# First attention of a four-layer kernel: the mixing matmuls go ahead of the scores, and GpSimd scales half of the probabilities

## The reference, cut to what matters

```
ln_out = ln(x)
q, k, v    = fp8-rounded linear of ln_out;  q, k per head of 128: layer norm     # "core"
qx         = fp8-rounded linear of ln_out, layer norm per head                    # "cross"
kx, vx     = linear of cond (fp32), kx: layer norm per head
scores = q . k / sqrt(128) ; p = softmax(scores) ; out = p . v                    # 16 heads, 8 key groups
cat = [core, xout] -> clamp, round to fp8 -> linear to 256 features               # added to x
```

## Time and profile before

| | |
|---|---|
| median of 3 runs | 1504.31 us |
| the profiled execution | 1502.7 us |
| its span | 1500.9 us |
| PE busy over the span | 1437.8 us (96%) |
| DVE / ACT / POOL busy | 877.0 / 768.6 / 526.4 us |
| first attention | from the start to about 460 us |

### The profile page before, as it was taken

One profiled execution on the slowest core, in us unless ns is written; L12 is line 12 of the kernel. 1 busy time (PEld: TensorE's weight loads), 2 busy tenths in 40 slices (PEclk: granted clock), 3 DMA queues, 4 the chain that ended last, 5 costly groups with the idle time before them and its releaser, 6 DMA issues. The chain is left out here.

```text
span 1500.9 us, 22370 instructions
## 1 busy us (share of the span) xinstructions
PE 1437.8 (96%) x7006; PEld 1040.2 (69%) x7006; DVE 877.0 (58%) x1923; ACT 768.6 (51%) x2123; POOL 526.4 (35%) x522
## 2 busy tenths in 40 slices
PE   6999999999989999999999999999997999999998
PEld 5677777788875555557878888866764666665656
DVE  5798988899875242333464545455677555553322
ACT  5888888999982211110234444444357655553210
POOL 2767677877761000000533333322111333321000
PEclk9999999999999999999999999999999999999999
DMA  5301000200006511112100000000232000011120
GB/s 204 118 6 64 5 5 1 97 1 1 2 1 265 180 53 49 49 50 91 67 1 1 0 1 1 15 15 6 102 150 97 1 1 1 1 30 43 47 69 17
DMA packets 21880, 71.67 MB, mean 48 GB/s; under 512 B 3922, under 2 KB 6354, under 8 KB 19076
## 3 DMA queue, kind: packets, MB, share of 16 engines
q1 hardware_dynamic: 13556, 57.38, 10.4%
q10 hardware_dynamic: 8208, 12.87, 2.8%
HBM read 69.01 MB, written 1.22 MB: 47 GB/s over the span
## 5 line engine op out<-in xcount | busy, mean ns | idle before, releaser
L1282 ACT ACTIVATE l0f_silu<-bank 128x512 f32<-128x512 f32 x48 | 28.5, 597 | 198.9 <-PE bank L1206 183.0
L948 POOL TENSOR_TENSOR l0a_head_rstd<-l0a_head_var,all_minus_half 128x4 f32<-128x4 f32 x96 | 99.6, 1042 | 18.2 <-DVE l0a_head_var L666 18.2
L1385 DVE TENSOR_TENSOR l0f_product<-l0f_silu,bank 128x512 f32<-128x512 f32 x48 | 32.9, 687 | 124.3 <-ACT l0f_silu L1282 124.2
L920 POOL TENSOR_TENSOR l0a_stepped<-l0a_y,l0a_m 128x512 f32<-128x512 bf16 x64 | 73.8, 1153 | 89.1 <-DVE l0a_m L644 87.5
L484 PEld LDWEIGHTS bank<-l0a_k_t,l0a_q_t 128*128 128x128 f32 x512 | 63.7, 191 | 39.7 <-ACT l0a_q_t L832 35.3
L846 ACT ACTIVATE l0a_work<-bank,l0a_neg_max 128x128 f32<-128x128 f32 x256 | 90.3, 372 | 1.2 <-DVE l0a_neg_max L679 1.2
L1218 PEld LDWEIGHTS bank<-all_weights_a,l0f_hidden 128*128 128x128 f32 x384 | 72.9, 190 | 25.3 <-issue 17.0
L1814 DVE TENSOR_TENSOR all_weights_a<-bank,all_cols 128x512 f32<-128x512 f32 x64 | 43.9, 690 | 77.6 <-PE bank L1649 46.2
L1218 PE MATMUL bank<-all_weights_a,l0f_hidden 128*128 128x256 f32 x384 | 88.9, 379 | 0.0
L2407 PE MATMUL bank<-l3a_f_xn_t,all_weights_b 128*128 128x512 f32 x192 | 86.2, 594 | 0.0
L890 ACT ACTIVATE l0a_work<-l0a_work,l0a_row_inv 128x128 f32<-128x128 f32 x256 | 82.4, 411 | 6.2 <-DVE l0a_row_inv L683 5.9
(11 more groups left out here) (443 smaller groups left out, 3760.3 us busy)
## 6 DMA issues: line engine op xcount, KB each, us to landing
l0f_spread<-l0f_weights ACTq DMA_DIRECT2D x32, 192.0 KB, 2.7
all_weights_a<-in_l_w_q SPq DMA_DIRECT2D x2, 2048.0 KB, 13.8
l0f_spread<-l0f_weights ACTq DMA_DIRECT2D x32, 128.0 KB, 2.8
all_weights_b<-in_l_e_gate_up SPq DMA_DIRECT2D x1, 3200.0 KB, 10.4
all_weights_b<-in_l_e_gate SPq DMA_DIRECT2D x1, 3072.0 KB, 10.0
all_weights_a<-in_l_e_up SPq DMA_DIRECT2D x4, 768.0 KB, 6.7
all_weights_a<-in_l_e_down SPq DMA_DIRECT2D x1, 3072.0 KB, 15.2
l3a_spread<-l3f_weights SPq DMA_DIRECT2D x10, 256.0 KB, 3.4
```

The costliest lines, as they stand in the source:

```text
L920: done = g.tensor_tensor(stepped[:, 0:n], value, step, ALU.add)
L948: g.tensor_tensor(head_rstd[:, m % 2, :], head_var[:, m % 2, :], res.minus_half[:, 0:HU], ALU.pow)\
```

## The change

Two edits. On PE, `mix` comes before `score` within the odd steps. And for a = 0 and a = 3 of every tile the scaling of the probabilities is one POOL instruction on 128 x 512, with `row_inv` broadcast along the row, in place of four ACT instructions. It keeps its step (s+6, that is step 7 for a = 0, and step 5 of the next tile for a = 3). ACT adds a wait for the count of POOL's scaling before that of a = 1.

```
+        POOL_SCALED = (0, 3)
...
-            march(VTS, STEPS, [(turn_probs, later(at_query, 7)), (score, later(at_query, 4)),
-                               (mix, later(at_query, 8)), in_tile(F_TILE, turn_first, F_TURN),
+            march(VTS, STEPS, [(turn_probs, later(at_query, 7)), (mix, later(at_query, 8)),
+                               (score, later(at_query, 4)), in_tile(F_TILE, turn_first, F_TURN),
...
             def scale_probs(b, a):                                   # ACT
+                if a in POOL_SCALED:
+                    return
                 inv_ready.wait(act, inv_ready.at(b, a + 1))
+                if a - 1 in POOL_SCALED:
+                    probs_ready.wait(act, probs_ready.at(b, a))
...
+            def scale_probs(b, a):                                   # POOL
+                if a not in POOL_SCALED:
+                    return
+                inv_ready.wait(g, inv_ready.at(b, a + 1))
+                probs_ready.wait(g, probs_ready.at(b, a))
+                pr = heads(probs[:, a % 2, :])
+                g.tensor_tensor(pr, pr, along(row_inv[:, a, :], P), ALU.mult).then_inc(probs_ready.sem, 1)
...
-            march(VTS, STEPS, [(round_mixed, later(at_query, 9)), (rstd, later(at_norm, 1)), in_tile(F_ROWS_TILE, first_rstd, F_ROWS[0:1]),
+            march(VTS, STEPS, [(round_mixed, later(at_query, 9)), (rstd, later(at_norm, 1)), (scale_probs, later(at_query, 6)),
+                               in_tile(F_ROWS_TILE, first_rstd, F_ROWS[0:1]),
                                in_tile(0, out_low_first, OUT_FIRST_LOW), (quantise, [4, 6, 8]),
```

## The result

The changed kernel took 1547.34 us (median of 4 runs, 1546.90 to 1551.51) against 1504.43 for the kernel before: ratio 1.0295, 95% interval 1.0274 to 1.0317, or +43 us where +38 was forecast. The profiled execution is the longest of the four, 1551.51 us, so its trace stands some 4 us behind the median.

What follows compares the result with a forecast made beforehand. PE was taken to bound the cross tiles and DVE's packed timeline the core tiles. Losses of 13 us (cross), 4.5 and 3.5 (tiles 8, 9), 15 (tiles 10 to 14) and 2 made +38, 1541 us; range 1512 to 1562.

Steps and rivals of the forecast that it cites:

- the timeline of DVE is packed: Core tiles: DVE runs from one rounding to the next without a wait, in a tile of 24.9 us.
- ACT's relief at nothing: Attention tiles: taking 2.6 us a tile from ACT gains nothing, since ACT is not the bound.
- rival (C): Attention tiles: ACT's load causes PE's waits for q_t, so less of it gains some 10 us, 1493 us; chance 0.08.
- The place of the scaling: Core tile, step 5: POOL's scaling of a = 3 starts right behind the quantising, takes 1.04 us, making PE 3.30 us late.
- PE's lateness: Core tile: late transposes delay step 7's row max by 3.1 us, so DVE stands still 2.7 us more.
- PE was to wait once a tile: Expected trace sign: PE's weight loads wait for POOL's new scaling once a tile, about 3 us.
- The hold: Core tiles: POOL's large instruction blocks DVE's 16-bit instructions, 0.6 us more a tile at most.
- The order at 0: Mix ahead of score on PE: taken as 0 in cross and core tiles, between 16 us lost and 10 gained.
- the 5.65 us: Core tile: time from PE's step 6 transposes to the earliest row max of step 7, in the new order.
- The bound of 16 us: Largest loss from mix ahead of score: 0.5 us on all 32 query units of the core tiles.
- The sum: First 460 us: 13 + 4.5 + 3.5 + 15 + 2 = +38 us, giving 1541 us; what follows unchanged.
- cross tiles 27.5: Expected trace sign: cross tiles take 27.5 us in the changed kernel.

Runs made afterwards that it cites:

- spare multiply: Kernel before plus an unread GpSimd multiply of the same size at the two new places, ScalarE still scaling: 1521.8 us, ratio 1.0119.
- scaling ahead of the quantising: GpSimd scales a = 0 and 3, score ahead of mix, two quantisings moved one step later, against the kernel before: 1523.4 us, ratio 1.0130.
- order alone: Kernel before with only mix put ahead of score on PE, all four scalings still on ACT: 1512.8 us, ratio 1.0062.
- wait alone: Kernel before plus an unread 4-column GpSimd power at the two places, PE's transposes of a = 0 and 3 waiting for it: 1531.6 us, ratio 1.0179.
- spare small instruction: Kernel before plus an unread GpSimd power of 128x4, about 1.0 us long, at the two new places: 1503.8 us, ratio 0.9998.
- relief alone: Kernel before with a = 0 and 3 scaled by no engine, PE's transposes of them waiting for the exponentials only: 1505.4 us, ratio 1.0014.
- scaling alone: Changed kernel without its second edit: GpSimd scales a = 0 and 3, score ahead of mix; against the kernel before 1534.5 us, ratio 1.0204.

## Why the prediction was right

**What bounds the kernel.** "In the core tile the timeline of DVE is packed" is true only with two things that I had not counted. Of the 24.9 us 3.4 are hold, so the list by itself is shorter. And there is a loop of the same length: DVE's rounding, POOL's two rounding instructions and rstd, DVE's normalise and next rounding, 6.2 us per query unit (375.74 to 381.90 in the earlier trace rows). Once in each core tile DVE waits for it, also in tile 13, just behind the stretch that I had read as free of waits:

```profile
385.46 0.69 DVE L674 TENSOR_TENSOR l0a_work<-bank,l0a_head_rstd 128x512 f32<-128x512 f32 x1 [0.32 <-POOL l0a_head_rstd L948]
```

With rstd 1.3 us earlier the tile is 1.2 us shorter, of which 0.8 is less hold and 0.3 fewer gaps. So whether the loop or DVE's held list sets the tile is open: in the kernel before they are within 0.3 us a tile of each other. A row without gaps doesn't tell whether the engine is full or fed just in time, nor does it show time lost inside instructions that are held.

**ACT's relief at nothing:** shown for the old order, 1.0014. The gain of rival (C) is not there even without POOL's scaling.

**The place of the scaling** and PE's lateness: shown. The scaling's start and duration are as forecast, and the row max of step 7 is 2.9 us late where 3.1 was forecast. The wait by itself costs 27 us. PE was to wait once a tile, about 3 us; in a core tile it waits twice, 1.81 and 1.31 us.

**The hold** was taken as "0.6 us more at most" a core tile and nothing in the cross tiles. In the changed kernel's core tiles it is 0.4 us, as forecast. With PE on time it is 1.7 us a core tile and 18 us in all (spare multiply), and in the scaling ahead of the quantising it is all that is left of a core tile's price (1.3 us). In the cross tiles it was left out without a reason.

**The order at 0** is the term that failed: 9 us alone, 13 beside the scaling. I had argued slack between score and row max; with the order alone DVE waits there in 29 places. Only its price beside a late scaling was in the sum, within the 5.65 us, and it is 0.9 us a core tile. The bound of 16 us holds as a number only: it was for the core tiles, and part of the 9 us arises in the cross tiles, which had "0".

**The sum.** In the core tiles 3.0 us was taken and 3.3 measured, and its parts, a DVE that stands still (2.7 taken, 2.8 measured) and a hold (0.6 at most, 0.4 measured), are those of the sum. From tile to tile: 13 us were forecast up to the seventh addition, 22.5 measured, of which 5.4 at the first, where I had 1.4; 17 from there to the twelfth, 15.7 measured; 8 for the rest, 9.8 measured. So the cross tiles and the fill carry the difference, and the sign "cross tiles 27.5" failed (29.4 measured): there hold and order stood at nothing, and by the eighth addition the order alone is 6.0 us late, the spare multiply 9.4, the wait alone 14.6. These three are of one trace each and rough: the spare small instruction and the relief, whose times are those of the kernel before, are 4.5 and 1.3 us late there too.

The mechanism of the loss in the core tiles was right. That the whole came within 5 us is partly luck: the cross tiles and the fill were priced 9.5 us too low and the last tiles 1.8 too low, the core tiles between them 1.3 too high, and the trace that shows this is itself 4 us longer than the median. The parts measured alone (9, 18 and 27 us) add up to 54 us for 43, an overlap that the sum did not price.

## What to carry to other kernels

Work moved to an idle engine starts where that engine's list lets it, not when its input is there: compare the end of what stands ahead of it with the start of its reader. A wide GpSimd instruction (128 x 512 here) also costs what VectorE's 16-bit instructions lose under it, so count those on the path that sets the tile. And before relieving an engine, leave the work out once: here this was no faster (ratio 1.0014), so the move had nothing to bring.

## What the runs showed that I had not expected

**PE's granted clock** was 1.00 over the first 500 us of the kernel before; in slower kernels it fell at times. (In the first 40 us it is 0.96 in the changed kernel, but also in the relief alone and the spare small instruction, which cost nothing.) In the kernel with the wait alone it fell in the core tiles too, as here at 325 us, just after PE had stood waiting 2.57 us for the transposes that began at 324.05. Three stretches of it (granted clock behind POOL's count) and scores in and out of one:

```profile
324.00:326.00 2.00, 1.92 (x15) 1.95 (x16) 1.75 (x5) 0.00 (x0) 1.71 (x2) 0.84 0.01 4
326.00:328.00 2.00, 2.00 (x7) 1.71 (x7) 0.78 (x1) 1.33 (x3) 1.84 (x3) 0.50 0.00 0
328.00:330.00 2.00, 2.00 (x13) 1.83 (x13) 0.46 (x1) 1.68 (x6) 1.86 (x3) 0.80 0.00 0
```

```profile
327.71 1.60 PEld L486 LDWEIGHTS bank<-l0a_k_t,l0a_q_t 128*128 128x128 f32 x8
...
339.75 0.97 PEld L486 LDWEIGHTS bank<-l0a_k_t,l0a_q_t 128*128 128x128 f32 x8 [0.44 <-ACT l0a_q_t L836]
```

0.50 is the lower level, 1.2 GHz, and the eight weight loads took 1.60 us there for 0.97. Over its first 500 us the granted clock is 0.97, in the changed kernel 0.99. So a part of the wait's 27 us may be clock, and the wait's price at the full clock lower than this run says; this may be one reason why the parts add up to more than the whole. From 300 to 460 us the clock was 0.94 with the wait alone and 0.97 with the scaling alone, but 1.00 in the changed kernel, so its core tiles' 28.2 us are not a matter of the clock. How much of the wait's price is clock was not tried.
